# Moving VectorE's two expert-number loads to behind the dense products of a pass, in a fused attention and mixture-of-experts kernel

## The chip, the cores and the metric

One Trainium2 chip, one of its cores. The time is device microseconds of one execution; a median of several runs is given with its lowest and highest. Everything below on the order of work is in terms of the core's engines: TensorE (PE, with PEld for its weight loads), VectorE (DVE), ScalarE (ACT), GpSimd (POOL) and SyncE (SP, which issues most DMAs). Each engine runs its own instruction stream, and engines wait for each other through semaphores.

## The reference, cut to what matters

Two layers over x of 8 x 100 tokens with 256 features: cross-attention and a top-1 mixture of experts, then cross-attention with normalised queries and keys and a top-8 mixture of 64 experts. The change touches only the last part:

```python
topk_idx, topk_w = _route(x, router_w, e_bias)          # 8 of 64 experts for each of 800 tokens
coef = jnp.zeros((T, E), topk_w.dtype).at[jnp.arange(T)[:, None], topk_idx].add(topk_w)
g = jnp.einsum('th,ehi->tei', x, Wg)
u = jnp.einsum('th,ehi->tei', x, Wu)
h = jax.nn.silu(g) * u * coef[:, :, None]
moe_out = jnp.einsum('tei,eih->th', h, Wd)
shared = jax.nn.silu(x @ SWg) * (x @ SWu) @ SWd
return (moe_out + shared).reshape(orig_shape)
```

## The kernel before

The kernel runs its stages one after the other: projections and attention of layer 0, its experts, projections and attention of layer 1, the routing and the shared expert, and last the 64 experts. That last stage is a loop over passes (two nested loops whose counter is `i`, with a number of passes that depends on the routing; in the profiled execution there are 8). A pass handles four experts. Two of them (`p` = 0, 1) are computed densely, for all 800 tokens in two halves of 400. The other two (`k` = 0, 1) are "small": at most 128 tokens each, which are gathered into rows, computed, and spread back. Every product is made of parts in reduced precision, a `high` and a `low` one that add up to the float32 value: `x_high`, `x_low`, `we_high`, `we_low` and so on. ScalarE writes the high part; GpSimd or VectorE subtracts it from the original to get the low part.

The order of the work is written out by hand, for each engine in a function of its own (`pe_experts1`, `act_experts1`, `pool_experts1`, `dve_experts1`, `sp_experts1`). There is no scheduler; an engine runs what stands in its function in that order and waits where a `wait_ge` says so.

TensorE in a pass: `gate_up` of dense expert 0 and 1 (L2169 to L2171; 24 matmuls each), `down` of expert 0 (L2181 to L2183) with the transposes of the small experts' rows between (L2191), then `small_gate_up` (L2200 to L2202), and then the rest of `down`, in turns with the small experts' remaining steps (L2207, L2211 to L2213, L2221). `small_gate_up` waits for the low part of the gathered rows, which VectorE writes:

```python
pe.wait_ge(small_step[k], SPREAD * (i + 1) + ROWS_LOW)
```

ScalarE in a pass: `silu` of each dense half in PSUM (L2280), `high` of each product (L2285), splits of weights (L2270, L2274, L2290), `take_rows` (L2294, `xsT_high`), and the small experts' silu and copies.

VectorE in a pass: `find_rows` (L2420 to L2423) turns the rank rows, which a DMA brings, into row numbers for the gather. Then for each dense half `hidden` makes two products: `g_act` (L2409; in the trace its output is called kT_all, the arena it lies in), which needs silu, and `h1T` (L2414; called v_all in the trace), which needs g_act. Between expert 0 and expert 1 `spread_rows` (L2427) builds the spreading matrices. Then come `rows_low` (L2432, `xsT_low`), `small_hidden` (L2436, `hs`), `hidden_low` (L2441) and `small_low` (L2446). `small_hidden` reads one column of the gathered rows, chosen by the number of the small expert. That number lies in `expert_list` in SBUF, and VectorE's sequencer reads it into a register with `value_load` (L2461), once for each of the two small experts. `small_at` gives its place in the list, an offset from the register `total`.

TensorE starts `gate_up` of the next dense expert only when the product h1T two halves earlier is done, since both use the same PSUM.

Of the kernel before, what the change touches and what calls it, by code (L numbers as in the profile page):

```python
# [29 lines left out]
def build(nc, a):  # L30
# [167 lines left out]
    E1, H1, HS = 64, 128, 256  # L198
# [23 lines left out]
    def carve_as(name, base, at, rows, n, dtype, floats):  # L222
        view = nc.alloc_sbuf_tensor_at(name, [rows, n], dtype, offset=base + 4 * at[0])[:, :]
        at[0] += floats
        return view
    expert_list = carve_as("expert_list", keys_at, at_k, 1, LISTED, I32, LISTED)
# [1650 lines left out]
    def small_at(e, total, i, k):  # L1877

        return nc.s_assert_within(total + 2 * i + k, 0, LISTED - 1, skip_runtime_bounds_check_because=
                                  "two more dense places than pairs, and two small ones to a pair")  # L1880
# [521 lines left out]
    def dve_experts1(dve):  # L2402
        def hidden(i, p):
            n = 2 * i + p
            for half in range(2):

                dve.wait_ge(coef_loaded[p], 16 * i + 16)
                dve.wait_ge(silu_done, 2 * n + half + 1)
                nc.vector.tensor_tensor(g_act[half], gu_ps[2 * half], coef_rows[p][:, half * HT:(half + 1) * HT], ALU.mult  # L2409
                                        ).then_inc(coef_used, 1)  # L2410
                dve.wait_ge(coef_used, 2 * n + half + 1 + 4)
                dve.wait_ge(gu_in_psum, 4 * n + 2 * half + 2 + 8)
                dve.wait_ge(h1_ready, 2 * n + half + 1)
                nc.vector.tensor_tensor(h1T[:, half * HT:(half + 1) * HT], g_act[half], gu_ps[2 * half + 1], ALU.mult  # L2414
                                        ).then_inc(h1_full, 1)

        def find_rows(i):
            for k in range(2):
                dve.wait_ge(rank_loaded[k], 16 * i + 16)
                nc.vector.scalar_tensor_tensor(matches[k], rank_rows[k], slot_col[:, 0:1], token_of, ALU.is_equal, ALU.mult,  # L2420
                                               accum_out=row_sum[:, k:k + 1]).then_inc(row_of_ready, 1)
            dve.wait_ge(row_of_ready, 3 * i + 2)
            nc.vector.tensor_copy(row_of, row_sum[:, 0:2]).then_inc(row_of_ready, 1)  # L2423

        def spread_rows(i, k):
            dve.wait_ge(small_step[k], SPREAD * i + SPREAD)
            nc.vector.tensor_scalar(spread[k], rank_rows[k], slot_col[:, 0:1], None, ALU.is_equal, ALU.add,  # L2427
                                    accum_out=row_sum[:, 2 + k:3 + k]).then_inc(spread_ready, 1)

        def rows_low(i, k):  # L2430
            dve.wait_ge(small_step[k], SPREAD * (i + 1) + ROWS_HIGH)
            nc.vector.tensor_tensor(xsT_low[k], xs_ps[k], xsT_high[k].bitcast(F32), ALU.subtract).then_inc(small_step[k], 1)  # L2432

        def small_hidden(i, k, e):
            dve.wait_ge(small_step[k], SPREAD * (i + 1) + SILU)
            nc.vector.scalar_tensor_tensor(hs[k], ss_act[k], x_rows[k][:, bass.ds(D + e, 1)], gus_ps[k][:, H1:2 * H1],  # L2436
                                           ALU.mult, ALU.mult).then_inc(small_step[k], 1)

        def hidden_low(i, k):
            dve.wait_ge(small_step[k], SPREAD * (i + 1) + HIDDEN_HIGH)  # L2440
            nc.vector.tensor_tensor(hsT_low[k], hsT_ps[k], hsT_high[k].bitcast(F32), ALU.subtract  # L2441
                                    ).then_inc(small_step[k], 1)

        def small_low(i, k):
            dve.wait_ge(small_step[k], SPREAD * (i + 1) + OUT_HIGH)
            nc.vector.tensor_tensor(os_low[k], os_ps[k], os_high[k].bitcast(F32), ALU.subtract).then_inc(small_step[k], 1)  # L2446

        dve.wait_ge(route_step, 4)
        dve.sem_inc(h1_full, 2)
        dve.sem_inc(coef_used, 4)  # L2450
        dve.sem_inc(spread_ready, 2)
        dve.wait_ge(consts_ready, N_SPARSE + 1)
        dve.wait_ge(route_step, 5)
        total = dve.value_load(n_used[0:1, 0:1], min_val=0, max_val=E1)
        with dve.Fori(0, E1 // (2 * PAIRS)) as o:
            with dve.If(2 * PAIRS * o < total):
                with dve.Fori(0, PAIRS) as j:
                    i = o * PAIRS + j
                    with dve.If(2 * i < total):
                        find_rows(i)  # L2460
                        small = [dve.value_load(expert_list[0:1, bass.ds(small_at(dve, total, i, k), 1)], min_val=0,  # L2461
                                                max_val=E1 - 1) for k in range(2)]
                        hidden(i, 0)
                        for k in range(2):
                            spread_rows(i, k)
                        hidden(i, 1)
                        for k in range(2):
                            rows_low(i, k)
                        for k in range(2):
                            small_hidden(i, k, small[k])  # L2470
                        for k in range(2):
                            hidden_low(i, k)
                        for k in range(2):
                            small_low(i, k)
        for k in range(4):
            dve.wait_ge(out_in_psum, k + 1)
            two = x[:, 2 * k + 1:2 * k + 3, :]
            nc.vector.tensor_tensor(two, two, out_ps[k], ALU.add).then_inc(x_final, 1)


    with nc.Block() as block:
# [34 lines left out]
        @block.vector  # L2516
        def _(dve):
            dve_project0(dve)
            dve_attend0(dve)
            dve_gate(dve)  # L2520
            dve_experts(dve)
            dve_project1(dve)
            dve_attend1(dve)
            dve_add1(dve)
            dve_route1(dve)
            dve_experts1(dve)
# [60 lines left out]
```

## Time and profile before

| | us |
|---|---|
| median of 3 runs | 735.03 |
| lowest, highest | 734.36, 736.12 |
| the profiled execution (one of the three) | 736.12 |
| its span, first to last instruction | 734.3 |
| TensorE matmuls busy in the span | 640.9 (87%) |
| VectorE busy | 392.7 (53%) |
| ScalarE busy | 400.3 (55%) |
| GpSimd busy | 241.6 (33%) |

The profile gives for each instruction its start, its length, and, where its engine sat idle before it, how long and which event ended that. "issue" as releaser means that the engine waited for nothing that the profile shows. Matmuls are pipelined: a row's length overlaps the next row's start, so the distance of two starts says more than a length. Instructions that only the sequencer of an engine executes (register operations, register loads, asserts) are listed under the engine's queue name, DVEq for VectorE, and do not count as busy time.

### The profile page before, as it was taken

How to read it: one execution, taken by the hardware profiler on the slowest of the kernel's cores; microseconds unless marked ns; L12 is line 12 of the kernel's file. 1: busy time of each engine (PE TensorE's matmuls, PEld its weight loads, DVE VectorE, ACT ScalarE, POOL GpSimd, SP SyncE). 2: the span in 40 equal slices, each digit the busy share in tenths (PEclk: the TensorE clock that was granted, in tenths of full speed). 3: DMA queues.
4: the chain of work that ended last, by engine and by line, in shares of the span. 5: the costliest groups of instructions: out<-in, count | busy, mean ns of one | idle time of the engine just before them, and what ended most of it. 6: DMA issues, size and time to landing. Idle time of an engine off the chain costs nothing.

```text
span 734.3 us, 15108 instructions
## 1 busy us (share of the span) xinstructions
PE 640.9 (87%) x4752; PEld 513.3 (70%) x4753; DVE 392.7 (53%) x1172; ACT 400.3 (55%) x952; POOL 241.6 (33%) x309
## 2 busy tenths in 40 slices
PE   3999889999751999998999899997686999999995
PEld 2876566666541888976878666665554999999995
DVE  5222567777633111128889644546593665666662
ACT  1454689989641333335766878675321455444442
POOL 5011455555217000011110000000133777787771
PEclk9999599999955999999999999998597899999999
DMA  6118000000085488312110100000106655554541
GB/s 146 45 33 272 2 2 2 2 2 2 2 264 211 142 264 298 112 34 80 43 42 1 46 5 1 2 1 1 45 1 170 167 150 159 159 141 144 145 109 45
DMA packets 66262, 64.09 MB, mean 87 GB/s; under 512 B 10360, under 2 KB 60053, under 8 KB 66086
## 3 DMA queue, kind: packets, MB, share of 16 engines
q1 hardware_dynamic: 61628, 57.03, 26.1%
q0 software_dynamic: 1824, 4.32, 2.3%
q10 hardware_dynamic: 2762, 2.11, 0.9%
q8 instruction: 28, 0.46, 0.3%
q14 instruction: 20, 0.16, 0.1%
HBM read 55.15 MB, written 8.29 MB: 86 GB/s over the span
## 4 chain that ended last, share of the span: by engine, by line
PE 66%; DVE 10%; ACT 10%; issue 5%; DMA 4%; POOL 3%; SPq 1%; DVEq 1%; POOLq 0%; ACTq 0%
ACT probs L768 4%; PE psum L1120 4%; PE psum L1107 4%; PE psum L2169 3%; PE psum L2221 3%; PE psum L2171 3%; PE psum L2170 3%; PE psum L616 3%; PE psum L630 3%; PE psum L1594 3%; PE psum L707 3%; PE psum L1616 3%; PE psum L1603 3%; DMA v_all<-in_L_ffn_W_dram 3%; PE psum L697 2%
## 5 line engine op out<-in xcount | busy, mean ns | idle before, releaser
L768 ACT ACTIVATE probs<-probs,negmax 100x361 f32<-100x361 f32 x128 | 68.9, 587 | 10.7 <-POOL probs L813 10.6
L821 DVE TENSOR_SCALAR_CACHE_REDUCE probs<-psum 100x361 f32<-100x361 f32 x128 | 60.7, 530 | 19.4 <-PE psum L697 19.4
L707 PEld LDWEIGHTS psum<-ident,probs 100*128 100x128 f32 (+1 forms) x384 | 40.4, 159 | 27.6 <-issue 20.4
L707 PE MATMUL psum<-ident,probs 100*128 100x100 f32 (+1 forms) x384 | 48.9, 266 | 11.2 <-ACT probsT L776 4.8
L1148 ACT ACTIVATE kT_all<-psum,kT_all 128x128 f32<-128x128 f32 x88 | 25.2, 369 | 51.4 <-PE psum L1107 51.4
L813 POOL TENSOR_SCALAR probs<-probs 100x722 f32<-100x722 f32 x64 | 50.5, 789 | 5.1
L2169 PE MATMUL psum<-xT_high,we_high 128*128 128x400 f32 x128 | 45.9, 358 | 6.0 <-DVE v_all L2414 6.0
L1107 PE MATMUL psum<-kT_all,v_all 128*128 128x128 f32 x352 | 43.4, 283 | 7.9 <-DMA v_all<-in_L_ffn_W_dram 3.2
L2350 POOL TENSOR_TENSOR we_low<-v_all,we_high 128x512 fp32r<-128x512 f32 (+1 forms) x34 | 45.1, 1347 | 14.9 <-ACT we_high L2274 12.8
L1107 PEld LDWEIGHTS psum<-kT_all,v_all 128*128 128x128 f32 x352 | 42.0, 198 | 10.9 <-issue 6.8
L2053 POOL TENSOR_TENSOR xT_low<-kT_all,xT_high 128x1600 fp32r<-128x1600 f32 x1 | 3.6, 3567 | 130.9 <-ACT xT_high L2030 130.9
L2170 PE MATMUL psum<-xT_low,we_high 128*128 128x400 f32 x128 | 45.0, 352 | 0.0
L2171 PE MATMUL psum<-xT_high,we_low 128*128 128x400 f32 x128 | 45.0, 352 | 0.0
L1120 PE MATMUL psum<-v_all,kT_all 128*128 128x256 f32 x176 | 39.9, 380 | 0.1
L1667 ACT ACTIVATE probs<-probs,negmax 100x362 f32<-100x362 f32 x64 | 37.6, 595 | 3.3 <-DVE negmax L1714 3.3
L2358 POOL TENSOR_TENSOR h_low<-v_all,h_high 128x400 fp32r<-128x400 f32 x32 | 33.7, 1054 | 13.1 <-ACT h_high L2285 13.1
L2285 ACT ACTIVATE h_high<-v_all 128x400 fp32r<-128x400 f32 x32 | 17.2, 538 | 37.0 <-DVE v_all L2414 37.0
L1120 PEld LDWEIGHTS psum<-v_all,kT_all 128*128 128x128 f32 x176 | 32.6, 190 | 4.4 <-issue 0.4
L1714 DVE CUSTOM_DVE_ANT_0 probs<-psum,ctx_nat 100x362 f32<-100x362 f32 x64 | 31.0, 529 | 7.4 <-issue 5.3
L2409 DVE TENSOR_TENSOR kT_all<-psum,kT_all 128x400 f32<-128x400 f32 x32 | 18.3, 573 | 28.0 <-ACT psum L2280 26.6
L697 PE MATMUL psum<-kT_all,qT_all 32*100 32x361 f32 x256 | 30.1, 542 | 3.6 <-DVE probs L821 2.0
L810 POOL TENSOR_SCALAR negmax<-row_top 100x2 f32<-100x2 f32 x64 | 14.1, 221 | 53.8 <-DVE probs L821 51.3
(425 smaller groups left out, 1692.9 us busy)
## 6 DMA issues: line engine op xcount, KB each, us to landing
v_all<-in_L_ffn_W_dram SPq DMA_DIRECT2D x16, 1024.0 KB, 7.8
kT_all<-coefT_dram SPq DMA_DIRECT2D x16, 400.0 KB, 3.8
v_all<-in_L_ffn_Wg_dram SPq DMA_DIRECT2D x34, 128.0 KB, 2.3
v_all<-in_L_ffn_Wu_dram SPq DMA_DIRECT2D x34, 128.0 KB, 2.5
v_all<-in_L_ffn_Wd_dram SPq DMA_DIRECT2D x34, 128.0 KB, 2.7
ctx_nat<-in_ctx_dram SPq DMA_DIRECT2D x16, 192.0 KB, 2.5
xs_dram<-zeros SPq DMA_DIRECT2D x1, 2048.0 KB, 7.7
ys_dram<-zeros SPq DMA_DIRECT2D x1, 1792.0 KB, 12.5
```

Of the source, the lines that this page charges most:

```text
L697: last = nc.tensor.matmul(psum[0:NQ, strip, 0:NKV], q0_all[at, r, c, b * NQ:(b + 1) * NQ], A0.kT[at, c, b * NKV:(b + 1) * NKV], start=True ...
L707: last = nc.tensor.transpose(pT_ps[0:rows[t], t, hh * NQ:(hh + 1) * NQ], probs[:, n % NPB, hh, t * P:t * P + rows[t]], ident[0:NQ, 0:NQ])
L768: last = nc.scalar.activation(row, row, ACT.Exp, bias=negmax[:, n % NPB, hh:hh + 1])
L813: nc.gpsimd.tensor_scalar(pair, pair, CLAMP, -CLAMP, ALU.min, ALU.max).then_inc(A0.clamped, 1)
L821: last = nc.vector.tensor_scalar(probs[:, n % NPB, hh, 0:NKV], psum[0:NQ, n % 2 * 2 + hh, 0:NKV], -CLAMP, None, ALU.max, ALU.max, accum_ou ...
L1107: last = nc.tensor.matmul(hid_ps[m // 4][:, m % 4, :], w1_e[p][:, c, m * P:(m + 1) * P], xsT[:, c, :], start=(c == 0), stop=(c == 1))
L1120: last = nc.tensor.matmul(ys_ps, hT[:, m, :], w2_e[p][:, m, :], start=(m == 0), stop=(m == HC - 1))
L1667: last = nc.scalar.activation(row, row, ACT.Exp, bias=negmax[:, n % NPB, hh:hh + 1], scale=-1.0, accum_out=sums[:, b % 2, 2 * s + hh:2 * s ...
L2169: nc.tensor.matmul(ps, we_high[p][:, col], xT_high[:, c, tok], start=(c == 0), stop=False)
L2170: nc.tensor.matmul(ps, we_high[p][:, col], xT_low[:, c, tok], start=False, stop=False)
L2171: last = nc.tensor.matmul(ps, we_low[p][:, col], xT_high[:, c, tok], start=False, stop=(c == 1))
L2350: nc.gpsimd.tensor_tensor(we_low[p][:, cols], we[p][:, cols], we_high[p][:, cols].bitcast(F32), ALU.subtract).then_inc(we_split, 1)
```

## The change

The two `value_load` of a pass move from behind `find_rows(i)` to behind `hidden(i, 1)`, in VectorE's function alone. The loaded registers are first used in `small_hidden`, which stands behind both places.

```diff
                         find_rows(i)
-                        small = [dve.value_load(expert_list[0:1, bass.ds(small_at(dve, total, i, k), 1)], min_val=0,
-                                                max_val=E1 - 1) for k in range(2)]
                         hidden(i, 0)
                         for k in range(2):
                             spread_rows(i, k)
                         hidden(i, 1)
+                        small = [dve.value_load(expert_list[0:1, bass.ds(small_at(dve, total, i, k), 1)], min_val=0,
+                                                max_val=E1 - 1) for k in range(2)]
                         for k in range(2):
                             rows_low(i, k)
```

VectorE's instructions at the old place, between the cast that ends `find_rows` and the first product of `hidden(i, 0)`; "ISA" rows are register and semaphore-threshold arithmetic or the bound asserts of a load, TENSOR_LOAD is a register load, and a minus marks what goes:

```order
 L2422 ISA
 L2423 CAST row_of<-row_sum 128x2
-L2461 ISA
-L2461 TENSOR_LOAD expert_list
-L2461 ISA x3
-L2461 TENSOR_LOAD expert_list
-L2461 ISA x2
 L2408 ISA
 L2409 TENSOR_TENSOR kT_all<-psum,kT_all 128x400
```

Eight instructions leave this place (two loads and six of arithmetic and asserts), and the cast is followed directly by the threshold arithmetic of L2408 and the first product.

VectorE's instructions at the new place, between the last product of `hidden(i, 1)` and the first `xsT_low`; line numbers with a plus are those of the changed file:

```order
 L2412 REGISTER_ALU
 L2414 TENSOR_TENSOR v_all<-kT_all,psum 128x400
+L2465 ISA
+L2465 TENSOR_LOAD expert_list
+L2465 ISA x3
+L2465 TENSOR_LOAD expert_list
+L2465 ISA x2
 L2431 ISA
 L2432 TENSOR_TENSOR xsT_low_88<-psum,xsT_high_82 128x256
```

The same eight instructions now stand between the last h1T product and the threshold arithmetic of L2431. The instruction streams of TensorE, ScalarE, GpSimd and SyncE are the same before and after.

## Rows read from the trace of the kernel before

Lines of the kernel are given as L and a number. Pass 0 begins at about 558 us, pass 1 at 586 us.

**Rows 1.** Busy time by stretch, then engine totals; columns as the first line says.

```profile
core 0: us, PE busy (x) PEld busy (x) DVE busy (x) ACT busy (x) POOL busy (x), PEclk, DMA share, GB/s
...
574.60:731.00 156.40, 150.19 (x881) 144.67 (x879) 92.49 (x189) 74.12 (x171) 112.77 (x96) 1.00 0.49 134
```

**Rows 2.** Timeline of TensorE (start, length, engine, line, operation), then its stretch.

```profile
562.42 0.34 PE L2170 MATMUL psum<-xT_low,we_high 128*128 128x400 f32 x1
562.60 0.34 PE L2171 MATMUL psum<-xT_high,we_low 128*128 128x400 f32 x1
568.92 0.70 PE L2169 MATMUL psum<-xT_high,we_high 128*128 128x400 f32 x1 [5.98 <-DVE v_all L2414]
569.42 0.54 PE L2170 MATMUL psum<-xT_low,we_high 128*128 128x400 f32 x1
569.75 0.54 PE L2171 MATMUL psum<-xT_high,we_low 128*128 128x400 f32 x1
...
567.80:574.40 6.60, 5.48 (x16) 5.43 (x17) 4.99 (x10) 3.38 (x6) 5.95 (x6) 0.50 0.76 205
```

**Rows 3.** VectorE in pass 0, then the loads' rows on its sequencer (565 to 568 us).

```profile
565.86 0.17 DVE L2423 CAST row_of<-row_sum 128x2 uint32<-128x2 f32 x1
567.51 0.57 DVE L2409 TENSOR_TENSOR kT_all<-psum,kT_all 128x400 f32<-128x400 f32 x1 [1.48 <-issue]
...
L2461 DVEq FUSED_REGOPS  x4: 71/137/218, 565.9 to 567.1; - x4
L2461 DVEq TENSOR_LOAD <-expert_list x2: 318/320/323, 566.0 to 566.8; - x2
L2461 DVEq SEQ_ASSERT  x2: 23/23/23, 566.6 to 567.3; - x2
```

**Rows 4.** Passes 1 and 2: VectorE, its sequencer's loads in pass 1, ScalarE.

```profile
586.37 0.58 DVE L2423 CAST row_of<-row_sum 128x2 uint32<-128x2 f32 x1
588.42 0.57 DVE L2409 TENSOR_TENSOR kT_all<-psum,kT_all 128x400 f32<-128x400 f32 x1 [1.48 <-ACT psum L2280]
...
608.11 0.57 DVE L2409 TENSOR_TENSOR kT_all<-psum,kT_all 128x400 f32<-128x400 f32 x1 [1.48 <-ACT psum L2280]
...
L2461 DVEq FUSED_REGOPS  x4: 64/137/225, 586.4 to 587.6; - x4
L2461 DVEq TENSOR_LOAD <-expert_list x2: 299/302/305, 586.5 to 587.3; - x2
L2461 DVEq SEQ_ASSERT  x2: 23/23/23, 587.1 to 587.8; - x2
...
587.90 0.49 ACT L2280 ACTIVATE psum<-psum 128x400 f32<-128x400 f32 x1 [3.68 <-PE psum L2171]
...
607.59 0.49 ACT L2280 ACTIVATE psum<-psum 128x400 f32<-128x400 f32 x1 [3.68 <-PE psum L2171]
```

**Rows 5.** Pass 1, around the new place: VectorE, then ScalarE.

```profile
596.28 0.57 DVE L2409 TENSOR_TENSOR kT_all<-psum,kT_all 128x400 f32<-128x400 f32 x1 [1.00 <-ACT psum L2280]
597.05 0.57 DVE L2414 TENSOR_TENSOR v_all<-kT_all,psum 128x400 f32<-128x400 f32 x1 [0.19 <-DVE kT_all L2409]
597.53 0.75 DVE L2432 TENSOR_TENSOR xsT_low<-psum,xsT_high 128x256 fp32r<-128x256 f32 x2
...
596.80 0.66 ACT L2294 ACTIVATE xsT_high<-psum 128x256 fp32r<-128x256 f32 x2 [0.55 <-PE psum L2191]
```

**Rows 6.** TensorE in front of L2200, in passes 1, 7 and 0.

```profile
597.56 0.34 PE L2182 MATMUL psum<-h_high,we_high 128*128 128x400 f32 x1
597.74 0.35 PE L2183 MATMUL psum<-h_low,we_high 128*128 128x400 f32 x1
598.19 0.36 PE L2200 MATMUL psum<-ws_high,xsT_high 128*128 128x256 f32 x1
...
715.90 0.34 PE L2183 MATMUL psum<-h_low,we_high 128*128 128x400 f32 x1
716.35 0.36 PE L2200 MATMUL psum<-ws_high,xsT_high 128*128 128x256 f32 x1
...
578.38 0.35 PE L2183 MATMUL psum<-h_low,we_high 128*128 128x400 f32 x1
578.56 0.31 PE L2200 MATMUL psum<-ws_high,xsT_high 128*128 128x256 f32 x1
```

**Rows 7.** VectorE in pass 0, around the new place.

```profile
576.40 0.57 DVE L2414 TENSOR_TENSOR v_all<-kT_all,psum 128x400 f32<-128x400 f32 x1 [0.19 <-POOL h_low L2358]
577.86 0.76 DVE L2432 TENSOR_TENSOR xsT_low<-psum,xsT_high 128x256 fp32r<-128x256 f32 x2 [0.88 <-ACT xsT_high L2294]
```

**Rows 8.** A stop of TensorE in an earlier stage, and its stretch.

```profile
317.66 0.57 PE L1107 MATMUL psum<-kT_all,v_all 128*128 128x128 f32 x3 [1.78 <-issue]
...
315.00:318.00 3.00, 1.22 (x8) 0.80 (x7) 0.42 (x1) 0.00 (x0) 0.00 (x0) 1.00 0.13 44
318.00:322.00 4.00, 4.00 (x37) 3.95 (x36) 0.27 (x1) 1.63 (x6) 0.00 (x0) 1.00 0.00 0
```


## The prediction

> **What bounds the kernel now.** I read the page first, for which engine is full, then one pass of the last loop in the timeline of each engine, then the sequencer's own rows for the two loads. The change touches only the last stage, the loop over pairs of experts (8 passes, from about 556 us to 726 us). There TensorE is the bound: from 574.6 us to 731 us it is busy 150.19 of 156.40 us, at a granted clock of 1.00, while VectorE is busy 92.49 us [rows 1]. A full pass takes 19.7 us: the last gate/up result of the first half becomes g_act at 588.42 us in pass 1 and at 608.11 us in pass 2 [rows 3, 4]. So only what makes TensorE wait changes the time. Inside the loop it waits for VectorE in two places. In pass 0 it stands still for 5.98 us until 568.92 us, waiting for the first product h1T (v_all, L2414) [rows 2]. In passes 1 to 7 it waits shortly in front of the small experts' gate/up (L2200): matmuls normally start 0.18 us apart (597.56 and 597.74), but L2200 starts 0.45 us after the last L2183 (597.74 to 598.19), so 0.27 us of waiting; the last pass shows the same, 715.90 to 716.35 [rows 6]. What L2200 waits for is xsT_low, which VectorE starts at 597.53, directly behind its last h1T product of 597.05 [rows 5]. Pass 0 has no such wait (578.38 to 578.56) [rows 6].
>
> **What the loads cost.** The block is two register loads with their address arithmetic and bound asserts. Its sequencer rows in pass 0: four register operations, two TENSOR_LOAD of 0.32 us, two asserts; first row at 565.9, last at 567.3 [rows 3]. Around it the cast starts at 565.86 and lasts 0.17, and g_act starts at 567.51 with 1.48 us of idle that nothing but issue ended [rows 3]. So from the start of the vector instruction ahead of the block to the start of the one behind it: 567.51 - 565.86 = 1.65 us; from its end: 1.48 us. Two facts on when it starts. It does not start before the instruction ahead of it starts: the cast at 565.86 or 586.37, the first register operation at 565.9 or 586.4. And it does not wait for that instruction to end: in pass 1 the first load starts at 586.5, while the cast runs from 586.37 for 0.58 us, to 586.95 [rows 4].
>
> **What the removal gives.** In passes 1 to 7: nothing. In pass 1 the block's last row starts at 587.8, but silu (L2280) runs from 587.90 to 588.39 and g_act starts at 588.42, 0.03 us behind it; pass 2 repeats it, 607.59 + 0.49 = 608.08 against 608.11 [rows 4]. The 1.48 us of idle looks like the price of the loads, but its releaser is silu, and silu waits for the matmuls. The loads lie in the shadow of TensorE there. In pass 0 silu was done long before (there the idle is put down to issue, not to silu [rows 3]), so g_act, h1T and the restart of TensorE come up to 1.48 us earlier. What survives of it depends on the clock. TensorE restarts at the lower level, 1.2 GHz: granted 0.50 from 567.8 to 574.4 us [rows 2]. There matmuls start 0.33 us apart (569.42, 569.75) against 0.18 at full clock (562.42, 562.60) [rows 2]. If the low stretch ends at the same instant, 1.48 us more time in it yields 1.48 x 0.18 / 0.33 = 0.81 us; if it ends as much earlier, 1.48 us. If it ends still sooner, the chain of VectorE and ScalarE holds: from g_act of the first half to xsT_low's neighbour h1T it needs 597.05 - 588.42 = 8.63 us [rows 4, 5]. With g_act at 566.03 that h1T starts at 574.66, xsT_low at 576.31, and L2200 follows 0.66 us behind it (598.19 - 597.53), at 576.97 against 578.56 today: 1.59 us gained at the most.
>
> **What the insertion costs.** The block now stands between the last h1T (L2414) and the first xsT_low (L2432). The semaphore arithmetic of L2431 stays behind it, as that of L2408 stood behind the block in pass 0. In passes 1 to 7 xsT_low then starts 1.65 us after h1T, at 597.05 + 1.65 = 598.70 instead of 597.53: 1.17 us later. ScalarE is no cover: both xsT_high begin at 596.80 and end at 597.46 [rows 5]. Nor has TensorE anything else queued in front of L2200; behind L2200 stand the remaining down matmuls and the small experts' whole tail. L2200 waits already, so all of the 1.17 us is added: its distance from L2183 grows from 0.45 to 1.62 us. Downstream everything is started by TensorE's results (silu of the small experts, hs, hsT, os), find_rows comes after them, and the next pass's g_act follows silu, which follows TensorE; nothing recovers the delay. 7 x 1.17 = 8.2 us. In pass 0 h1T starts at 576.40 and xsT_low at 577.86, after 0.88 us of waiting for ScalarE's xsT_high [rows 7]; 576.40 + 1.65 = 578.05, so 0.19 us later relative to the rest. L2200 had no spare there, so 0.19 is added.
>
> **The bounds of the insertion.** Below: the block's own rows, whose last start is 1.4 us after the first in both passes [rows 3, 4], could leave some 0.04 us less; say 1.13. Above: if a load there waits for the end of the vector instruction ahead of it, the price is 1.48 us behind h1T's end at 597.62, so 599.10 and 1.57 us later. I take 1.17, since in pass 1 the loads ran under a cast of the same 0.57 to 0.58 us as h1T. SP, GpSimd and ScalarE do not read the two registers, and their queues are unchanged. VectorE's own queue behind the block holds xsT_low, hs, hsT_low, os_low and then the next pass.
>
> **The sum.** Pass 0: between -0.81 + 0.19 = -0.6 and -1.6; I take -1.0, near the middle, because the trace does not say when the clock would come back. Passes 1 to 7: +8.2 (7.9 to 11.0). Together +7.2. The profiled execution took 736.12 us with its span of 734.3 us, and is the highest of the three: it would become 743.3. On the median of 735.03, which I predict against, **742.2 us**.
>
> **Rivals.**
> A. The sequencer runs ahead: the block is executed while the g_act ahead of it still waits for silu (1.00 us of idle in front of 596.28, from 595.28 on) [rows 5]. 595.28 + 1.48 = 596.76 lies before 597.53, so the insertion costs nothing and only pass 0 counts: 735.03 - 1.0 = 734.0. Against it: the cast too waits for the products ahead of it, and the block starts right behind the cast's start, not sooner, in passes 0 and 1 [rows 3, 4]. 5%. The Trainium skill states this as its rule (Advanced Engine Details and Errata, Sequencer Loop): the sequencer pushes an engine's instruction into a queue, where it waits for its semaphores, and goes on itself to control instructions. By that rule the time would be A's; the trace's rows do not agree with it here.
> B. The loads are what holds g_act in every pass, not silu. Then the chain to xsT_low starts up to 1.48 us earlier, which outweighs 1.17 and takes away the wait of 0.27 us: 735.03 - 7 x 0.27 - 1.0 = 732.1. It needs silu to end 1.4 us ahead of g_act. Rows 4 have it 0.03 us ahead. 4%.
> C. The clock falls. A wait of 1.6 us per pass might drop TensorE to 1.2 GHz. The low stretch of pass 0 holds 16 starts at 0.33 instead of 0.18 us, 2.5 us; seven of them give 742.2 + 17 = 759. Against it: TensorE stood still for 1.78 us until 317.66 and the granted clock stayed 1.00 [rows 8]. For it: in this loop the 5.98 us stop does lead into a low stretch [rows 2], and nothing here shows 1.6 us repeated every 20 us. 4%.
> D. The load waits for the end of h1T: 1.57 us in each of seven passes, 11.0 - 1.0, gives 745.0. 7%.
>
> **How the numbers follow.** The forecast has 80%: 742.2, with its own range of 741.3 (7.9 - 1.6) to 742.8 (8.3 - 0.6), widened by half of the 1.76 us between the lowest and highest of the three runs, some 0.9 us each way: 740.4 to 743.7. To take D in, the upper end goes to 745.2. Outside stay A, B and C with 13%. What a measurement of this kernel can tell from no change is about 0.2%, 1.5 us. B is faster (and a part of A), A within, the forecast, C and D slower: 5%, 4%, 91%.
>
> **What would show it.** Right: g_act in passes 1 to 7 still 0.03 us behind silu; xsT_low 1.65 us behind the start of h1T; L2200 starting 1.6 us after L2183; a pass of 20.9 instead of 19.7 us; in pass 0 the stop shortened from 5.98 to about 4.5 us. Wrong: loads that start before h1T (A), a pass that stays at 19.7 us, a granted clock under 1.00 between 575 us and the end (C), or xsT_low 2.05 us behind h1T's start (D).

## The result and the profile after

| | before, us | after, us |
|---|---|---|
| median (6 runs each) | 734.68 | 741.70 |
| lowest, highest | 734.22, 736.12 | 740.90, 742.68 |
| profiled execution | 736.12 | 740.93 |
| its span | 734.3 | 739.1 |

The changed kernel is slower by 7.0 us, a ratio of 1.0094 with a 95% interval of 1.0081 to 1.0107. The prediction was 742.2 us in a range of 740.4 to 745.2, with 91% on slower.

The top of the page of the changed kernel shows where the time is not: no engine is busier for it. VectorE is busy 393.2 us where it was 392.7, since the loads run on its sequencer and do not count as busy.

```profile
span 739.1 us, 15108 instructions
## 1 busy us (share of the span) xinstructions
PE 637.7 (86%) x4752; PEld 511.1 (69%) x4753; DVE 393.2 (53%) x1172; ACT 400.0 (54%) x952; POOL 240.9 (33%) x309
```

What grew is the waiting of TensorE in the last loop. The stretch view from 570 us, behind the slow start of pass 0, to 736 us answers [rows 1]: as before, a granted clock of 1.00, but 15.2 us without a matmul instead of 6.2.

```profile
core 0: us, PE busy (x) PEld busy (x) DVE busy (x) ACT busy (x) POOL busy (x), PEclk, DMA share, GB/s
570.00:736.00 166.00, 150.83 (x883) 145.11 (x881) 94.25 (x193) 74.53 (x171) 115.33 (x98) 1.00 0.47 129
```

At the old place nothing changed in passes 1 to 7. The timeline of VectorE (g_act of the first half in passes 1 and 2) and of ScalarE (the silu in front of the first) answers [rows 4]: silu ends at 584.77 + 0.49 = 585.26 us and g_act starts at 585.29, 0.03 us behind it, and the same idle of 1.48 us stands in front of it although no load is there any more. So that idle had never been the price of the loads. A pass takes 606.12 - 585.29 = 20.83 us, where it took 19.69.

```profile
585.29 0.57 DVE L2409 TENSOR_TENSOR kT_all<-psum,kT_all 128x400 f32<-128x400 f32 x1 [1.48 <-ACT psum L2280]
...
606.12 0.57 DVE L2409 TENSOR_TENSOR kT_all<-psum,kT_all 128x400 f32<-128x400 f32 x1 [1.48 <-ACT psum L2280]
...
584.77 0.49 ACT L2280 ACTIVATE psum<-psum 128x400 f32<-128x400 f32 x1 [3.68 <-PE psum L2171]
```

At the new place, in pass 1, the timeline of VectorE, its sequencer's rows for the loads and the timeline of TensorE answer [rows 5, 6]:

```profile
593.92 0.57 DVE L2414 TENSOR_TENSOR v_all<-kT_all,psum 128x400 f32<-128x400 f32 x1 [0.19 <-DVE kT_all L2409]
595.55 0.76 DVE L2432 TENSOR_TENSOR xsT_low<-psum,xsT_high 128x256 fp32r<-128x256 f32 x2 [1.06 <-issue]
...
L2465 DVEq FUSED_REGOPS  x4: 64/137/225, 594.0 to 595.2; - x4
L2465 DVEq TENSOR_LOAD <-expert_list x2: 304/306/307, 594.1 to 594.8; - x2
L2465 DVEq SEQ_ASSERT  x2: 23/23/23, 594.7 to 595.4; - x2
...
594.61 0.34 PE L2183 MATMUL psum<-h_low,we_high 128*128 128x400 f32 x1
596.22 0.36 PE L2200 MATMUL psum<-ws_high,xsT_high 128*128 128x256 f32 x1 [1.26 <-DVE xsT_low L2432]
```

xsT_low starts 1.63 us behind the start of h1T (593.92 to 595.55), where it was 0.48. The block's first row (594.0) stands just behind the start of h1T, and its first load at 594.1, 0.4 us before h1T ends at 594.49. L2200 starts 1.61 us behind the last L2183 (594.61 to 596.22), where it was 0.45, and the profile now names the wait, 1.26 us for xsT_low.

Pass 0 answers [rows 2, 7]: TensorE, then VectorE, then TensorE in front of L2200.

```profile
560.69 0.34 PE L2171 MATMUL psum<-xT_high,we_low 128*128 128x400 f32 x1
565.84 0.70 PE L2169 MATMUL psum<-xT_high,we_high 128*128 128x400 f32 x1 [4.80 <-DVE v_all L2414]
566.34 0.54 PE L2170 MATMUL psum<-xT_low,we_high 128*128 128x400 f32 x1
566.67 0.54 PE L2171 MATMUL psum<-xT_high,we_low 128*128 128x400 f32 x1
...
568.67 0.54 PE L2171 MATMUL psum<-xT_high,we_low 128*128 128x400 f32 x1
569.00 0.39 PE L2169 MATMUL psum<-xT_high,we_high 128*128 128x400 f32 x1
569.23 0.34 PE L2170 MATMUL psum<-xT_low,we_high 128*128 128x400 f32 x1
...
573.07 0.57 DVE L2414 TENSOR_TENSOR v_all<-kT_all,psum 128x400 f32<-128x400 f32 x1 [0.19 <-DVE kT_all L2409]
574.73 0.76 DVE L2432 TENSOR_TENSOR xsT_low<-psum,xsT_high 128x256 fp32r<-128x256 f32 x2 [1.09 <-issue]
...
574.25 0.34 PE L2183 MATMUL psum<-h_low,we_high 128*128 128x400 f32 x1
575.39 0.36 PE L2200 MATMUL psum<-ws_high,xsT_high 128*128 128x256 f32 x1 [0.80 <-DVE xsT_low L2432]
```

TensorE stands still for 4.80 us instead of 5.98. In VectorE's rows of this profile the cast starts at 564.32 and g_act at 564.43 us, 0.11 us apart where it was 1.65; counted from the first matmul of the pass, the cast itself, which stands behind a wait for rank rows from a DMA, came 0.36 us later than before. TensorE restarts at the lower clock (starts 0.33 us apart) but is back at 0.18 us from 569.23 on, 3.4 us after its restart; before, the low stretch went on until 574.4, 5.5 us after it. Against that, L2200 of pass 0 now waits 0.80 us, 1.14 us behind L2183, where it had not waited at all.

The balance of the two profiled executions, from the first matmul of each pass: pass 0 took 586.51 - 558.08 = 28.43 us before and 583.38 - 556.18 = 27.20 us after, 1.23 us less. Passes 1 to 7 take 7 x 1.14 = 8.0 us more. Together 6.8 us, against 7.0 between the medians. (The spans differ by less, 4.8 us, since pass 0 itself began 1.9 us earlier in the profiled execution after: in the stages ahead of it the code is the same. Every figure for one pass is from one profiled execution of a kernel.)

### The profile page after: what moved, and what is told of

It reads as the page before. It is cut to its first block, busy times and chain, and to the rows that moved or that the text cites. A ratio compares the mean times of both kernels' runs of the same rounds, so it can differ in the third digit from the quotient of the medians.

```text
span 739.1 us, 15108 instructions
## 1 busy us (share of the span) xinstructions
PE 637.7 (86%) x4752; PEld 511.1 (69%) x4753; DVE 393.2 (53%) x1172; ACT 400.0 (54%) x952; POOL 240.9 (33%) x309
## 4 chain that ended last, share of the span: by engine, by line
PE 61%; DVE 11%; ACT 11%; issue 6%; DMA 4%; POOL 3%; DVEq 2%; SPq 2%; ACTq 0%; POOLq 0%
ACT probs L768 4%; PE psum L1120 4%; PE psum L1107 4%; PE psum L2221 3%; PE psum L616 3%; PE psum L630 3%; PE psum L1594 3%; PE psum L1616 3%; PE psum L2169 3%; PE psum L2171 3%; PE psum L2170 3%; PE psum L1603 3%; DMA v_all<-in_L_ffn_W_dram 3%; PE psum L707 2%; PE psum L1642 2%
```

## The experiments

My theory was that the loads cost nothing at the old place in passes 1 to 7, because they lay beside TensorE's and ScalarE's work, and their whole length at the new one, because L2200 waits for the very next instruction. The rivals were A (the sequencer runs them ahead), B (they held g_act everywhere) and C (the clock falls). Eight kernels moved, removed or repeated the loads. Each diff below is cut, and shows what was added against the kernel before; where loads stand at another place, those of the old place are gone, except in the run with the block twice at the old place. All times are medians; "pass" is the distance of the first matmuls of passes 1 and 2; the last column is the start of L2200 less that of the L2183 ahead of it, in pass 1. "Pass 0" is from its first matmul to that of pass 1. In the first group of four the kernel before had a median of 734.78 us in 24 runs (732.18 to 736.94), in the second 734.41 in 23 runs (731.46 to 737.4).

| kernel | us | ratio to before, 95% | pass 0 | pass | L2200 |
|---|---|---|---|---|---|
| before | 734.68 | | 28.43 | 19.69 | 0.45 |
| changed | 741.70 | 1.0094 (1.0081 to 1.0107) | 27.20 | 20.83 | 1.61 |
| no loads | 731.70 | 0.9949 (0.9929 to 0.9968) | 25.83 | 19.6 | 0.51 |
| one at each place | 736.62 | 1.0025 (1.0009 to 1.0041) | 26.22 | 20.1 | 0.83 |
| twice at the new place | 758.17 | 1.0318 (1.0291 to 1.0346) | 27.6 | 22.1 | 2.85 |
| three at the new place | 749.70 | 1.0220 (1.0193 to 1.0248) | 27.6 | 21.5 | 2.22 |
| twice at the old place | 741.53 | 1.0104 (1.0084 to 1.0124) | 29.14 | 20.5 | 1.29 |
| between the halves | 733.41 | 0.9984 (0.9969 to 1.0000) | 25.65 | 19.7 | 0.50 |
| behind rows_low | 732.88 | 0.9971 (0.9956 to 0.9986) | 26.11 | 19.7 | 0.51 |
| ahead of find_rows | 733.16 | 0.9991 (0.9976 to 1.0005) | 26.35 | 19.7 | 0.52 |

### The removal alone: no loads

```diff
-                        small = [dve.value_load(...) for k in range(2)]
...
-                            small_hidden(i, k, small[k])
+                            small_hidden(i, k, 0)
```

> The two loads of a pass are left out, at both places; every small expert's coefficient column is the first one, so the small experts' weights are those of another expert and the time alone is meant. This is the removal without the insertion. My theory: at the old place the loads lie behind TensorE and silu in passes 1 to 7, so a pass stays at 19.7 us, with g_act still 0.03 us behind silu, L2200 still 0.45 us behind L2183, and only pass 0 gains, about 1.2 us: 734.7 - 1.2 = 733.5 (732.9 to 734.1). Rival B (the loads hold g_act in every pass): a pass of 19.4 us, and 7 x 0.27 us more are gained, 731.6. A third view, that the loads cost 1.48 us in every pass wherever they stand, would give 734.7 - 8 x 1.48 = 722.9.

Measured: 731.70 us. The timeline of VectorE shows g_act in passes 1 and 2, that of ScalarE the silu of pass 1; then come xsT_low and hs of VectorE in pass 2.

```profile
584.83 0.57 DVE L2409 TENSOR_TENSOR kT_all<-psum,kT_all 128x400 f32<-128x400 f32 x1 [1.52 <-ACT psum L2280]
...
604.44 0.57 DVE L2409 TENSOR_TENSOR kT_all<-psum,kT_all 128x400 f32<-128x400 f32 x1 [1.52 <-ACT psum L2280]
...
584.31 0.49 ACT L2280 ACTIVATE psum<-psum 128x400 f32<-128x400 f32 x1 [3.68 <-PE psum L2171]
...
613.56 0.75 DVE L2432 TENSOR_TENSOR xsT_low<-psum,xsT_high 128x256 fp32r<-128x256 f32 x2
615.52 0.35 DVE L2436 SCALAR_TENSOR_TENSOR hs<-ss_act,x_rows,psum 128x128 f32<-128x128 f32 x1 [1.21 <-ACT ss_act L2298]
```

The row of hs in pass 1 of the kernel before:

```profile
599.61 0.35 DVE L2436 SCALAR_TENSOR_TENSOR hs<-ss_act,x_rows,psum 128x128 f32<-128x128 f32 x1 [1.33 <-ACT ss_act L2298]
```

g_act stands 0.03 us behind silu's end (584.80 to 584.83), with an idle of 1.52 us in front of it, although no load exists in this kernel. The time alone would speak for rival B: 731.70 us is B's figure (731.6) and lies below my range, 1.8 us under my 733.5. The rows decide against B: without loads g_act still waits for silu, L2200 still stands 0.51 us behind L2183, where B takes its wait away, and a pass is 19.6 us, not 19.4. The view that the loads cost 1.48 us in every pass is out by 9 us. Of the 1.8 us, about half is in the passes, 19.61 us (584.83 to 604.44) instead of 19.69, and later ones 19.57: hs starts 1.96 us behind xsT_low, where it was 2.08 (597.53 to 599.61). The run also replaced the register in the address of hs by a constant. In the kernel before, hs starts 0.15 us behind the end of ss_act (599.46 to 599.61), here 0.03 us (615.49 to 615.52), and TensorE's wait of 0.21 us for hs in front of L2207 is gone: 0.12 us a pass, 0.8 in all. So this run removed a little more than the loads. The rest is pass 0, which in the profiles gained 2.6 us instead of 1.2.

### One load at each place

```diff
                         find_rows(i)
+                        small0 = dve.value_load(...)
...
                         hidden(i, 1)
+                        small1 = dve.value_load(...)
```

> One load stays at the old place, one goes to the new one. If the price is so much for each load, the block of one takes about 0.75 us less than that of two (first register operations at 565.9, second load 0.8 us behind the first), so xsT_low starts 1.65 - 0.75 = 0.90 us behind the start of h1T instead of 0.48: 0.42 us in each of seven passes, 2.9; pass 0 gains about half of 1.2: 734.7 + 2.9 - 0.6 = 737.0 (736.2 to 737.8), L2200 0.87 us behind L2183. If the price is for any block of loads at the new place (a drained engine, say), passes cost 1.13 us as in the changed kernel: 734.7 + 7.9 - 0.6 = 742.0.

Measured: 736.62 us. VectorE, then TensorE, pass 1:

```profile
595.17 0.57 DVE L2414 TENSOR_TENSOR v_all<-kT_all,psum 128x400 f32<-128x400 f32 x1 [0.19 <-DVE kT_all L2409]
596.02 0.76 DVE L2432 TENSOR_TENSOR xsT_low<-psum,xsT_high 128x256 fp32r<-128x256 f32 x2 [0.29 <-issue]
...
595.86 0.34 PE L2183 MATMUL psum<-h_low,we_high 128*128 128x400 f32 x1
596.69 0.36 PE L2200 MATMUL psum<-ws_high,xsT_high 128*128 128x256 f32 x1 [0.49 <-DVE xsT_low L2432]
```

xsT_low starts 0.85 us behind h1T and L2200 0.83 us behind L2183; the theory had 0.90 and 0.87. The price goes by the load, not by the block: one load adds 0.37 us to the spacing of 0.48, the second 0.78. The first adds less because most of it lies under h1T, which runs until 595.74; its rows on the sequencer start at 595.2 (the register arithmetic), 595.3 (the load) and 595.9 us (the last assert). The time came close to the 737.0 with one part off: pass 0 gained 2.2 us in the profile, not 0.6.

### The same block twice at the new place

```diff
                         hidden(i, 1)
+                        small = [dve.value_load(...) for k in range(2)]
+                        again = [dve.value_load(...) for k in range(2)]
```

> The block of two loads stands twice at the new place (the second pair is not used), none at the old place. If the block lies wholly on the path there, each pass, pass 0 too, takes 1.46 us more than in the changed kernel, and L2200 starts 3.1 us behind L2183: 741.7 + 8 x 1.46 = 753.4. If the sequencer could run part of it beside other work, less: with a queue ahead of it, near 741.7. Rival C (the clock): with the wait now some 2.7 us in each pass the granted clock may fall, and each pass in which it does takes up to 2.5 us more, up to 773. I expect 1.00 from pass 1 on.

Measured: 758.17 us, 4.8 us over the theory. The second pair costs less than I said, 1.25 us (L2200 at 2.85 instead of 1.61 us), and its rows show one register operation for each load instead of two. With that price the sum would be 741.7 + 8 x 1.25 = 751.7 us, so 6.5 us remain. In the profiled execution, which took 756.91 us, 1.3 less than the median, the clock accounts for 4.4 of them. TensorE in pass 2 (its wait for xsT_low), then the stretches of passes 1 and 2:

```profile
622.27 0.36 PE L2200 MATMUL psum<-ws_high,xsT_high 128*128 128x256 f32 x1 [2.49 <-DVE xsT_low L2432]
...
587.00:609.00 22.00, 19.29 (x114) 18.62 (x113) 12.39 (x25) 9.71 (x22) 15.28 (x13) 1.00 0.50 132
609.00:632.00 23.00, 20.51 (x113) 19.96 (x112) 12.24 (x25) 9.62 (x22) 15.23 (x14) 0.93 0.45 126
```

Pass 1 keeps a granted clock of 1.00 and takes 22.1 us. In pass 2 the mean is 0.93 and it takes 23.1 us. Four of the passes 1 to 7 have a low stretch (2, 4, 5 and 6); they take 1.0 us more than pass 1, one of them 1.3. I had expected 1.00 from pass 1 on and was wrong; rival C's mechanism exists, at a wait of 2.5 us.

### Three loads: does the clock fall here too?

```diff
                         hidden(i, 1)
+                        small = [dve.value_load(...) for k in range(2)]
+                        third = dve.value_load(...)
```

> Three loads at the new place (the third a repeat that is not used). With four, L2200 came 2.85 us behind L2183 and TensorE's granted clock fell for a while in several passes; with two it is 1.60 us and the clock stays. A repeated load took 0.62 us, so L2200 comes 2.2 us behind L2183. If the clock holds: 8 x 0.62 = 5.0 over the changed kernel's 741.7, 746.7, a pass of 21.45 us. If it falls as with four loads, some passes take 1 us more, and the time is 748 to 752. I expect that it holds (60 to 40).

Measured: 749.70 us. VectorE in pass 2; TensorE in front of L2200 in pass 3; then three stretches around that wait:

```profile
617.90 0.57 DVE L2414 TENSOR_TENSOR v_all<-kT_all,psum 128x400 f32<-128x400 f32 x1 [0.19 <-DVE kT_all L2409]
620.16 0.76 DVE L2432 TENSOR_TENSOR xsT_low<-psum,xsT_high 128x256 fp32r<-128x256 f32 x2 [1.68 <-issue]
...
640.04 0.34 PE L2183 MATMUL psum<-h_low,we_high 128*128 128x400 f32 x1
642.25 0.36 PE L2200 MATMUL psum<-ws_high,xsT_high 128*128 128x256 f32 x1 [1.87 <-DVE xsT_low L2432]
...
621.60:643.00 21.40, 19.32 (x114) 18.66 (x113) 12.37 (x25) 9.71 (x22) 15.27 (x14) 1.00 0.50 137
643.00:646.40 3.40, 3.40 (x15) 3.21 (x14) 0.99 (x4) 1.04 (x4) 1.08 (x1) 0.50 0.53 152
646.40:668.00 21.60, 19.50 (x114) 18.82 (x114) 12.27 (x26) 9.67 (x22) 15.32 (x13) 1.00 0.48 134
```

xsT_low stands 2.26 us behind h1T, 0.63 more for the third load, as expected. TensorE waits 1.87 us, and then, from 643.0 to 646.4 us, works at a granted clock of 0.50. This happened in two of the passes 1 to 7 and made them 22.5 instead of 21.45 us. So my 60-to-40 guess that it holds was wrong. In the changed kernel, with a wait of 1.26 us, no pass had it.

### Twice at the old place: how large is the shadow?

```diff
                         find_rows(i)
                         small = [dve.value_load(...) for k in range(2)]
+                        again = [dve.value_load(...) for k in range(2)]
```

> The block of two loads stands twice at the old place (the second pair is not used), none at the new one. My theory says that the old place has a shadow of limited size: in pass 2 of the kernel before the cast starts at 606.05, the block would let g_act start at 607.69, and silu ends at 608.08, so 0.4 us are spare. A second pair took 1.25 us in the run with the block twice at the new place. So g_act comes 1.25 - 0.4 = 0.85 us later in passes 1 to 7, the chain to xsT_low with it, and L2200 starts 1.3 us behind L2183; a pass of 20.5 us. 7 x 0.85 = 5.9, and about 1 us in pass 0: 734.8 + 6.9 = 741.7 (740.5 to 743). If VectorE's products were not the chain that sets xsT_low, the extra would vanish: 735.8. If the first block already lay on the path (rival B), 734.8 + 8 x 1.25 = 744.8.

Measured: 741.53 us (expected 741.7). VectorE in pass 2, the cast and g_act; ScalarE, the silu between them:

```profile
608.11 0.58 DVE L2423 CAST row_of<-row_sum 128x2 uint32<-128x2 f32 x1
610.95 0.57 DVE L2409 TENSOR_TENSOR kT_all<-psum,kT_all 128x400 f32<-128x400 f32 x1 [2.27 <-ACT psum L2280]
...
609.64 0.49 ACT L2280 ACTIVATE psum<-psum 128x400 f32<-128x400 f32 x1 [3.68 <-PE psum L2171]
```

Now silu ends at 610.13 and g_act comes at 610.95, 0.82 us later (0.85 expected): here, and not in the kernel before, the loads hold it, though the profile's releaser still reads ACT. The delay travels along VectorE's and ScalarE's chain to xsT_low, L2200 starts 1.29 us instead of 0.45 behind L2183, and a pass takes 20.5 us. So in these passes the old place covers the two loads and 0.4 us more.

### Between the two halves

```diff
                 for half in range(2):
+                    if p == 1 and half == 1: small[:] = [dve.value_load(...) for k in range(2)]
                     dve.wait_ge(coef_loaded[p], 16 * i + 16)
```

> The loads stand inside hidden(i, 1), between the two halves: behind h1T of the first half, ahead of g_act of the second, where VectorE of the kernel before waits 1.00 us for silu. This is only some 2.3 us ahead of the changed kernel's place, on the same chain. If only what exceeds the idle is paid: the first-half h1T starts at 594.71 in pass 1, 1.65 us later is 596.36, against 596.28 for g_act: 0.08 us a pass, 0.6 in all, less the gain of pass 0: 732.9 + 0.6 = 733.5 (732.8 to 734.5). If a load on the products' chain costs wherever it stands, 741. L2200 0.5 to 0.6 us behind L2183.

Measured: 733.41 us. VectorE in pass 2 (lines past 2406 are three higher here): the first half's h1T, g_act, h1T, xsT_low.

```profile
612.13 0.57 DVE L2417 TENSOR_TENSOR v_all<-kT_all,psum 128x400 f32<-128x400 f32 x1 [0.20 <-DVE kT_all L2412]
613.75 0.57 DVE L2412 TENSOR_TENSOR kT_all<-psum,kT_all 128x400 f32<-128x400 f32 x1 [1.04 <-ACT psum L2280]
614.51 0.57 DVE L2417 TENSOR_TENSOR v_all<-kT_all,psum 128x400 f32<-128x400 f32 x1 [0.19 <-DVE kT_all L2412]
615.00 0.75 DVE L2435 TENSOR_TENSOR xsT_low<-psum,xsT_high 128x256 fp32r<-128x256 f32 x2
```

From h1T to g_act it is 1.62 us, with the loads between; without them it was 1.57 (594.71 to 596.28). The same block, 2.3 us ahead of the changed kernel's place and on the same chain, costs 0.05 us a pass instead of 1.14. The idle there waits for silu, and the loads lie beside it. The time, 733.41 us, is what that theory gave (733.5); the other view, that a load on the products' chain costs wherever it stands, had 741.

### Behind rows_low

```diff
                         for k in range(2):
                             rows_low(i, k)
+                        small = [dve.value_load(...) for k in range(2)]
                         for k in range(2):
                             small_hidden(i, k, small[k])
```

> The loads stand one step further back, between rows_low (xsT_low) and small_hidden (hs), where VectorE of the kernel before waits 1.33 us for ss_act. If what costs is the place ahead of L2200's wait and not the loads as such, nothing is added in passes 1 to 7: the second xsT_low starts at about 597.9 in pass 1 of the kernel before, 1.65 us later is 599.55, and hs starts at 599.61. Pass 0 gains as in the changed kernel: 734.7 - 1.2 = 733.5 (732.7 to 734.4), a pass of 19.7 us. If the loads cost anywhere behind the products, 741 to 742. Between them: the 0.06 us of spare may be overdrawn by 0.1 us a pass, 734.2.

Measured: 732.88 us, a ratio of 0.9971 (0.9956 to 0.9986): faster than the kernel before, and than the changed one by 8.8 us. VectorE in pass 2, TensorE in front of L2200 in the same pass, and TensorE's restart in pass 0:

```profile
614.09 0.57 DVE L2414 TENSOR_TENSOR v_all<-kT_all,psum 128x400 f32<-128x400 f32 x1 [0.19 <-DVE kT_all L2409]
614.58 0.75 DVE L2432 TENSOR_TENSOR xsT_low<-psum,xsT_high 128x256 fp32r<-128x256 f32 x2
616.64 0.35 DVE L2436 SCALAR_TENSOR_TENSOR hs<-ss_act,x_rows,psum 128x128 f32<-128x128 f32 x1 [1.31 <-ACT ss_act L2298]
...
614.77 0.34 PE L2183 MATMUL psum<-h_low,we_high 128*128 128x400 f32 x1
615.23 0.36 PE L2200 MATMUL psum<-ws_high,xsT_high 128*128 128x256 f32 x1
...
567.17 0.45 PE L2169 MATMUL psum<-xT_high,we_high 128*128 128x400 f32 x1 [4.63 <-issue]
```

hs starts 2.06 us behind xsT_low, as before (2.08), and the idle of 1.31 us in front of it is put down to ss_act; the loads lie in it. L2200 is back at 0.46 us, and in pass 0 TensorE stands still for 4.63 us instead of 5.98. One step further back in the program than the changed kernel, the block is free again, and pass 0 keeps its gain.

### Ahead of find_rows

```diff
+                        small = [dve.value_load(...) for k in range(2)]
                         find_rows(i)
```

> The loads stand at the head of a pass, ahead of find_rows. In pass 0 VectorE waits 9.5 us for the rank rows there, so they are free and pass 0 gains as with the loads behind rows_low. In passes 1 to 7 find_rows, the cast and with them the gather come some 1.6 us later, and g_act still finds silu later than itself (the cast would start near 607.2 to 607.6 of pass 2, silu ends at 608.08). Theory: a pass of 19.7 us, 732.9 (732.3 to 734.0). Rival: the later gather makes GpSimd's queue late (h_low, ws_low stand behind it), and L2200 or the down matmuls wait for ws_low: up to 1 us a pass, 740.

Measured: 733.16 us, a ratio of 0.9991 (0.9976 to 1.0005), not told from the kernel before. The pass stays at 19.7 us and L2200 at its distance, so the rival with the late gather is out: there too the loads are hidden in passes 1 to 7. In pass 2 the cast starts at 605.35 us and g_act at 606.39, with 0.88 us of idle put down to silu: what VectorE loses ahead of find_rows it makes up in the wait for silu behind it.

## Why the prediction was right

**The bound.** Right. The loop goes by TensorE, and the only waits that moved are the two named: pass 0's restart and L2200.

**The removal gives nothing in passes 1 to 7.** Right, and shown twice: the idle of 1.48 us stands unchanged where the loads left, and the run without loads has 1.52 us there. The step rested on silu's end 0.03 us ahead of g_act [rows 4]. The run with the block twice at the old place measured the spare there, 0.4 us, as worked out from the cast.

**The insertion costs 1.17 us in each of seven passes.** The mechanism was right and the size too: 1.14 measured (8.0 us instead of 8.2). xsT_low came 1.63 us behind h1T's start instead of 1.65. That the block runs under the vector instruction ahead of it, which decided against the upper bound of 1.57, holds in the changed kernel's rows. Rival D is out.

**Pass 0: -1.0.** Measured -1.23, inside -0.6 to -1.6, but its two terms were mis-sized and cancelled, so that this part of the sum came out by luck. g_act moved up against the cast as said (1.65 to 0.11 us). But the removal gave more than was counted: with the loads behind rows_low pass 0 takes 26.11 us, 2.3 less than before. I had bounded it by 1.59, from g_act advanced by 1.48 us and the vector chain's length to L2200 with the loads at their new place; without them there L2200 is free to come 1.2 us sooner. The early end of the low stretch, the open term, came true. The insertion cost more too: not 0.19 us but about 1 (27.20 - 26.11 = 1.1; L2200 at 1.14 instead of 0.18 us behind L2183). The 0.19 counted on the 0.88 us of slack in [rows 7]. In the two profiles with two or more loads at the old place xsT_low stands 1.45 to 1.46 us behind h1T in pass 0, but in the four with early clock and no load at the new place only 0.65 to 0.74 us: with TensorE fast again the slack was mostly gone.

The profiles part into two groups. Counted from the first matmul of pass 0, TensorE restarted at 8.8 to 9.7 us and its starts were back to 0.18 us apart at 12.8 to 13.6 us in all eight kernels with fewer than two loads between find_rows and hidden; in the kernel before and the one with the block twice there it restarted at 10.8 and 11.8 us, and was back at 16.3 and 16.9 us. Whether the restart's moment decides that was not tested by itself, and one profile for each kernel does not show how much pass 0 varies from execution to execution. The medians warn of it. For the seven kernels that stay at a granted clock of 1.00 in passes 1 to 7, pass 0 and seven passes added up from the profiles make them 0.2 to 1.5 us better against the kernel before than the medians do (between the halves: -2.5 against -1.0 us). So pass 0 of the kernel before may have been longer in its profile than in most of its executions, and the gains of 2.1 to 2.8 us that the table shows in pass 0 for five of the kernels may be about 1 us too large.

**The rivals.** A is out: the block starts right behind the start of the vector instruction ahead of it in the changed kernel as before, and every load added at the new place came out in the time. The order in which the sequencer would leave a waiting instruction behind and go on to the loads, which the Trainium skill describes (Advanced Engine Details and Errata, Sequencer Loop), is not what these rows show for a register load. B is out. C did not happen at a wait of 1.26 us, but is real: at 1.87 us two of seven passes had it, at 2.5 us four. I had given it 4% and an argument from one stop of 1.78 us that did not lower the clock [rows 8]; that argument was weak, for with a block only 0.6 us longer the time was 3.0 us above what a steady clock would give (749.70 against 746.7). Its price was wrong the other way: a pass with a low stretch took 1.0 us more, once 1.3, and not 2.5.

**The sum.** +7.2 predicted, +7.0 measured. The seven passes carry it by their mechanism; that pass 0 came within 0.3 us of its -1.0 is the luck told above. The upper end of the own range, 742.8, was worked out with 8.3 where the sum has 8.2; it changes nothing.

## What to carry to other kernels

An idle stretch with sequencer work in it does not by itself show a cost: here the same idle stayed when the work was taken out. Nor does the releaser's name decide it, which was ACT even where the loads held g_act; the distance from that releaser's end does, 0.03 us where the loads were wholly hidden and 0.82 us where they were not. Sequencer work belongs where its engine waits for another engine's data anyway. Moving it away from an early place frees nothing in the passes where it was hidden, and behind the last product nearly all of it stood on the path. Look for a wait behind the block that is as long as the block: the three other places tried here had one, the last 0.05 us of it missing between the halves.

## What the runs showed of the hardware that I had not expected

- One register load between h1T and xsT_low added 0.37 us to their spacing, the second 0.78 us, a third that repeats an address 0.63 us. The first is cheap because most of it runs under the vector instruction ahead of it; the repeated one shows one register operation where the others show two. TENSOR_LOAD itself is 0.30 to 0.32 us in the rows of all of them.
- An operand addressed through a register costs something itself: hs started 0.15 us behind the end of ss_act, with a constant column 0.03 us.
- A wait of TensorE of 1.87 us in each pass of 21.5 us was followed by a stretch at 1.2 GHz in two of seven passes, and one of 2.5 us in four of seven; 1.26 us per pass of 20.8 us in none. This is one profiled execution of each.
- In pass 0 of five profiles TensorE, after standing still for 4.15 to 4.63 us, restarted at full clock and fell to the lower one within about 1.2 us. With the loads behind rows_low it restarted at 567.17 us, and its starts were 0.33 us apart from 567.64 to 570.97 us.
